# Attention block with resizing, one NeuronCore: the values of three batches in half-precision parts

## What is computed

```python
out = bilinear_resize(x, 64, 64)                       # 4096 positions, 256 channels
out = relu(bn(conv1x1(out, conv1_w), bn1_s, bn1_b))    # called a in the kernel
q, k = conv1x1(out, q_w, q_b), conv1x1(out, k_w, k_b)  # 32 channels each
v = conv1x1(out, v_w, v_b)                             # 256 channels
attn = softmax(einsum('bdi,bdj->bij', q, k), axis=-1)  # 4096 x 4096
out = gamma * einsum('bcj,bij->bci', v, attn) + out
out = bn(conv1x1(relu(bn(out, bn2_s, bn2_b)), conv2_w), bn3_s, bn3_b)
return relu(bilinear_resize(out, 128, 128) + x)
```

## Time and profile before

| | |
|---|---|
| median of 3 executions | 2367.78 us |
| the profiled execution | 2371.97 us |
| its span in the profile | 2370.2 us |
| granted TensorE clock, mean | 0.994 of full speed |
| PE busy | 2298.5 us (97%) |
| DVE busy | 1783.7 us (75%) |
| ACT busy | 1706.3 us (72%) |
| POOL busy | 1671.0 us (70%) |

### The profile page before, as it was taken

How to read it: one execution, slowest core, us unless ns; L and a number is a source line. 1 busy time by engine, 2 the same in 40 slices (tenths; PEclk the granted TensorE clock), 3 DMA queues, 4 the chain that set the end, 5 groups by cost and what they waited for, 6 DMA issues and landing times.

```text
span 2370.2 us, 48197 instructions
## 1 busy us (share of the span) xinstructions
PE 2298.5 (97%) x15970; PEld 1650.3 (70%) x15970; DVE 1783.7 (75%) x3294; ACT 1706.3 (72%) x3305; POOL 1671.0 (70%) x1610
## 2 busy tenths in 40 slices
PE   4799999999999999999999999999999999999998
PEld 2377777777667777777747777777775777777774
DVE  7666578887568888888657888888756777777778
ACT  5567777777657777777755777777765777777773
POOL 7992468888369988888728988889845454444464
PEclk8899999999999999999999999999999999999999
DMA  6321112322102332222301322233310112222322
GB/s 212 107 72 46 36 54 107 106 92 104 54 23 103 108 107 103 93 105 98 107 10 54 109 106 102 102 107 106 106 55 1 63 63 71 71 71 71 142 96 100
DMA packets 59273, 204.11 MB, mean 86 GB/s; under 512 B 8752, under 2 KB 9840, under 8 KB 59120
## 3 DMA queue, kind: packets, MB, share of 16 engines
q1 hardware_dynamic: 41696, 138.93, 18.2%
q10 hardware_dynamic: 17424, 63.45, 6.5%
HBM read 135.24 MB, written 67.11 MB: 85 GB/s over the span
## 4 chain that ended last, share of the span: by engine, by line
PE 88%; DVE 4%; ACT 3%; POOL 3%; issue 1%; SPq 1%; DMA 0%; DVEq 0%; ACTq 0%; POOLq 0%
PE acc L1139 19%; PE acc L1141 18%; PE acc L1140 18%; PE et L1015 10%; PE emx L1003 6%; PE wrk L1037 4%; PE acc L1065 4%; PE wrk L1003 3%; PE acc L1057 2%; PE wrk L1028 1%; DVE qs L768 1%; DVE ks L768 1%; PE acc L1049 1%; ACT qs L535 1%; ACT qs L534 1%
## 5 line engine op out<-in xcount | busy, mean ns | idle before, releaser
L1139 PE MATMUL acc<-vh,ph 128*128 128x257 f16 x4096 | 1120.1, 273 | 1.7 <-DVE vl L778 1.4
L1141 PE MATMUL acc<-vh,pl 128*128 128x257 f16 x4096 | 1116.2, 273 | 0.0
L1140 PE MATMUL acc<-vl,ph 128*128 128x256 f16 x4096 | 1110.9, 271 | 0.0
L463 ACT ACTIVATE ph<-et 128x512 f16<-128x512 f32 x1024 | 610.5, 596 | 301.8 <-PE et L1015 293.0
L727 DVE TENSOR_TENSOR pl<-et,ph 128x512 f16<-128x512 f32 x1024 | 700.6, 686 | 139.4 <-ACT et L464 135.8
L464 ACT ACTIVATE et<-et 128x512 f32<-128x512 f32 x1024 | 607.0, 593 | 0.0
L1140 PEld LDWEIGHTS acc<-vl,ph 128*128 128x128 f16 x4096 | 400.9, 98 | 277.4 <-issue 20.5
L1139 PEld LDWEIGHTS acc<-vh,ph 128*128 128x128 f16 x4096 | 400.2, 98 | 70.6 <-issue 11.0
L1141 PEld LDWEIGHTS acc<-vh,pl 128*128 128x128 f16 x4096 | 395.4, 97 | 56.2
L377 POOL TENSOR_TENSOR ct<-cd,uw 128x512 f32<-128x512 f32 x246 | 325.0, 1343 | 134.7 <-DVE xres L758 130.3
L1015 PE MATMUL et<-qs,ks 98*128 (+1 forms) x1024 | 390.2, 381 | 2.7 <-DVE pl L727 0.9
(11 more groups left out here) (142 smaller groups left out, 2673.0 us busy)
## 6 DMA issues: line engine op xcount, KB each, us to landing
xres<-in_x SPq DMA_DIRECT2D x139, 512.0 KB, 4.5
out<-xres ACTq DMA_DIRECT2D x121, 512.0 KB, 2.6
xin<-in_x SPq DMA_DIRECT2D x110, 512.0 KB, 3.7
xr<-in_x SPq DMA_DIRECT2D x7, 512.0 KB, 7.4
out<-xr SPq DMA_DIRECT2D x6, 512.0 KB, 2.6
out<-xr SPq DMA_DIRECT2D x2, 256.0 KB, 2.1
osb<-in_L_conv_conv_w SPq DMA_DIRECT2D x1, 256.0 KB, 7.7
osb<-in_L_conv_v_w SPq DMA_DIRECT2D x1, 256.0 KB, 7.8
```

The costliest lines, as they stand in the source:

```text
L463: ops.activation(ph[:, t % 4, :], et[t % 2][:, :], ACT.Exp)
L1139: mm(acc[it][:, 0:C + 1], ph[:, tt % 4, pt], vh[:, tt, 0:C + 1], start=tt == 0, stop=False)
L1140: mm(acc[it][:, 0:C], ph[:, tt % 4, pt], vl[:, tt, :], start=False, stop=False)
L1141: last = mm(acc[it][:, 0:C + 1], pl[:, tt % 4, pt], vh[:, tt, 0:C + 1], start=False, stop=tt == JT - 1)
```

## The change

For batches 2 to 4 (b = 1 to 3) the values are no longer float32 products. ACT writes a half-precision high part of the scaled `a` (`a_high`, two instructions of 512 columns per chunk, behind the chunk's second `conv1_out`), DVE the low part (`a_low`, two instructions, behind the last `max` unit of the step; that of chunk 7 behind the last `max` unit of all). Both lie in `xr`, over the rows that `conv1` has used. `values` then makes three half-precision products where there was one of float32. The scale of `a` has to be known before `a` is: it is bounded from the largest input row value. DVE takes the maxima of `xr` in the last block of a batch (`largest_z`, 8 instructions of 1024 elements at the steps of `T_Z`), PE sums over partitions at step 29 (`T_SIZE`), DVE works out the scale (`size_of_a`). The parts of the weights (`wvh`, `wvl`) and constants are made once, in batch 0, block 1, step 2 (`fixed_sizes`). POOL and the loads of the last shortcut rows wait for `values` before they write into `xr`. Names that are new: `a_part(ck, low, half)` is the place in `xr`.

```diff
             def blk(b, n, c):
                 if is_last(b, c):
-                    sp.wait_ge(c1_rdy, 2 * NB * B)
+                    sp.wait_ge(v_rdy, VU * B)
...
             # POOL, blk
+                        if j == 0 and b > 0:
+                            pool.wait_ge(v_rdy, b * VU + 2 * (n + 1))
                         dst = xr[:, bass.ds(n, 1), j % 2, (j // 2) * (DR // 2):(j // 2 + 1) * (DR // 2), :]
...
             # ACT
+            def a_high(b, ck):
+                if ck == 0:
+                    act.wait_ge(a_rdy, b)
+                for half in range(CH):
+                    last = ops.activation(a_part(ck, 0, half), a[:, half, ck * IB:(ck + 1) * IB], ACT.Copy,
+                                          scale=a_scale[:, half:half + 1])
+                last.then_inc(a_hi, 1)
...
                         conv1_out(b, i // 2, i % 2)
+                        if i % 2 and not is_first(b):
+                            act.wait_ge(c1_done, b * (2 * NB) + (i + 1))
+                            a_high(b, i // 2)
                         if i == 1 and not is_first(b):
                             for half in range(2):
                                 relu_h(b * NB - 1, half)
...
             # DVE
+            def a_low(b, ck):
+                dve.wait_ge(a_hi, (b - 1) * NB + (ck + 1))
+                for half in range(CH):
+                    last = ops.scalar_tensor_tensor(a_part(ck, 1, half), a[:, half, ck * IB:(ck + 1) * IB],
+                                                    a_scale[:, half:half + 1], a_part(ck, 0, half), ALU.mult, ALU.subtract)
+                last.then_inc(a_lo, 1)
+            def fixed_sizes():
+                for m, w in ((wv_max, wvt), (w1_max, w1t)):
+                    ops.tensor_reduce(m, w[:], AX.X, ALU.max, apply_absolute_value=True).then_inc(a_fixed, 1)
+                for m, i in ((abs_s, S1), (abs_b, B1)):
+                    ops.scalar_tensor_tensor(m, par[:, i, :], -1.0, par[:, i, :], ALU.mult, ALU.max).then_inc(a_fixed, 1)
...
+                for h in range(CH):
+                    ops.tensor_scalar(wvh[:, h, :], wvt[:, h, :], wv_inv[:, h:h + 1], None, ALU.mult).then_inc(a_fixed, 1)
+                dve.wait_ge(a_fixed, 8)
+                for h in range(CH):
+                    last = ops.scalar_tensor_tensor(wvl[:, h, :], wvt[:, h, :], wv_inv[:, h:h + 1], wvh[:, h, :], ALU.mult,
+                                                    ALU.subtract)
+                last.then_inc(a_known, 1)
+            def largest_z(b, ck):
+                dve.wait_ge(down_p, down_count(b + 1, PIECES * (ck + 1)))
+                ops.tensor_reduce(z_max[:, ck, :], xr[:, ck].rearrange("p h r c -> p h (r c)"), AX.X, ALU.max,
+                                  apply_absolute_value=True).then_inc(z_seen, 1)
...
+                    if g == 1 and t == T_FIXED:
+                        fixed_sizes()
+                    if c == NB - 1 and b < B - 1:
+                        if t in T_Z:
+                            largest_z(b, T_Z.index(t))
+                        if t == T_Z[-1]:
+                            size_of_z(b)
+                        if t == T_SIZE + 1:
+                            size_of_a(b)
...
             # PE
             def values(b, v):
+                if not is_first(b):
+                    pe.wait_ge(a_lo, (b - 1) * NB + (v // 2 + 1))
+                    if v == 0:
+                        pe.wait_ge(a_known, 1)
                 for jj in range(VB):
...
                     for h in range(CH):
+                        if not is_first(b):
+                            high, low = (a_part(jt // IT, i, h)[:, keys] for i in range(2))
+                            mm(out, high, wvh[:, h, :], start=h == 0, stop=False)
+                            mm(out, high, wvl[:, h, :], start=False, stop=False)
+                            last = mm(out, low, wvh[:, h, :], start=False, stop=h == CH - 1)
+                            continue
...
+                    if c == NB - 1 and t == T_SIZE and not (isinstance(b, int) and b == B - 1):
+                        pe.wait_ge(y_rdy, g * 2)
+                        pe.wait_ge(z_rdy, b + 1)
+                        for h in range(CH):
+                            last = mm(wrk[:, C + 1:C + 2], ones_p[:, :], z_all[:, h:h + 1], start=h == 0, stop=h == CH - 1)
+                        last.then_inc(z_sum, 1)
...
             # _sequence
-        seq += first + second + m[:3] + middle + m[3:] if vector else first + m[:2] + middle + m[2:3] + second + m[3:]
+        low = [("a_low", ck - 1)] if ck else []
+        seq += first + second + m[:3] + middle + m[3:] + low if vector else first + m[:2] + middle + m[2:3] + second + m[3:]
...
-        seq += [row, m[0], m[1], one, scale, m[2], qk, v[0], m[3], m[4], m[5], v[1], m[6], v[2], m[7], *v[3:6]]
+        seq += [row, m[0], m[1], one, scale, m[2], qk, v[0], m[3], m[4], m[5], v[1], m[6], v[2], m[7], ("a_low", NB - 1), *v[3:6]]
...
+T_FIXED = 2
+T_Z = (1, 3, 7, 10, 12, 19, 20, 26)
+T_SIZE = 29
```

More of the change, by code:

```diff
@@ L80, in attention_block_kernel @@
         w2t = sb("w2t", [P, CH, C])
+        wvh = sb("wvh", [P, CH, C], F16)
+        wvl = sb("wvl", [P, CH, C], F16)
+        zs = sb("zs", [P, 18])
+        wv_max, w1_max, wv_inv, abs_s, abs_b, z_all, a_scale = (zs[:, 2 * i:2 * i + 2] for i in range(7))
+        a_gain, a_rest, a_top, v_scale = (zs[:, 14 + i:15 + i] for i in range(4))
+        a_parts = sb("a_parts", [P, CH, 2])
+        z_max = sb("z_max", [P, NB, CH])
+        a_inv = sb("a_inv", [P, 1])
         wva = sb("wva", [P, CH, C])
@@ L206, in late_bank, with a_part @@
             return acc[i % 2 * 2 + part]
+        def a_part(ck, low, half):
+            return xr[:, ck].rearrange("p h r c -> p (h r c)").bitcast(F16)[:, (low * CH + half) * IB:(low * CH + half + 1) * IB]
         def last_bank(half):
@@ new lines, in size_of_a @@
+            def size_of_a(b):
+                dve.wait_ge(z_sum, b + 1)
+                if b == 0:
+                    dve.wait_ge(a_sum, 1)
+                    ops.tensor_scalar(zs[:, 14:16], wrk[:, C + 2:C + 4], 1e-30, None, ALU.max).then_inc(a_known, 1)
+                    dve.wait_ge(a_known, 2)
+                ops.tensor_scalar(a_top, wrk[:, C + 1:C + 2], a_gain, a_rest, ALU.mult, ALU.add).then_inc(z_step, 1)
+                dve.wait_ge(z_step, b * 4 + 2)
+                ops.reciprocal(a_inv[:], a_top).then_inc(z_step, 1)
+                dve.wait_ge(z_step, b * 4 + 3)
+                ops.tensor_scalar(a_scale, wv_max, a_inv[:], A_TOP, ALU.mult, ALU.mult).then_inc(a_rdy, 1)
+                ops.tensor_scalar(a_top, a_top, 1.0 / A_TOP, None, ALU.mult).then_inc(z_step, 1)
@@ L787, in enter @@
                         qk_low(b, i)
+                    elif kind == "a_low" and not is_first(b):
+                        a_low(b, i)
                     elif kind == "max":
@@ L968, in _ @@
             pe.wait_ge(size_part, 1)
-            mm(acc[3][:, 4 * D:4 * D + 2], ones_d[:, :], ws[:, :], start=True, stop=True).then_inc(size_sum, 1)
+            mm(acc[3][:, 4 * D:4 * D + 2], ones_p[0:D, :], ws[:, :], start=True, stop=True).then_inc(size_sum, 1)
             pe.wait_ge(wt_ok, 3)
@@ L1061, in values @@
             def values(b, v):
+                if not is_first(b):
+                    pe.wait_ge(a_lo, (b - 1) * NB + (v // 2 + 1))
+                    if v == 0:
+                        pe.wait_ge(a_known, 1)
                 for jj in range(VB):
                     jt = v * VB + jj
+                    out = acc[bank_of("values", v)][:, jj * C:(jj + 1) * C]
+                    keys = slice(jt % IT * P, (jt % IT + 1) * P)
                     for h in range(CH):
+                        if not is_first(b):
+                            high, low = (a_part(jt // IT, i, h)[:, keys] for i in range(2))
[3 more added lines that the diff above has]
+                            continue
                         last = mm(acc[bank_of("values", v)][:, jj * C:(jj + 1) * C], a[:, h, jt * P:(jt + 1) * P], wvt[:, h, :],
@@ L1166, in blk @@
                         shift_transposes(g + 1)
+                    if c == NB - 1 and t == T_SIZE and not (isinstance(b, int) and b == B - 1):
[4 more added lines that the diff above has]
+                        last.then_inc(z_sum, 1)
+                        if is_first(b):
+                            pe.wait_ge(a_size, 1)
+                            for h in range(CH):
+                                last = mm(wrk[:, C + 2:C + 4], ones_p[:, :], a_parts[:, h, :], start=h == 0, stop=h == CH - 1)
+                            last.then_inc(a_sum, 1)
             def batch(b):
```

29 lines of the change are left out of this document (25 added, 4 removed).

## The result

The changed kernel takes 2382.68 us (median; 2379.75 to 2384.51) against 2368.63 (2367.7 to 2370.28) for the kernel before, run beside it on the same chip: ratio 1.0055, interval 1.0043 to 1.0067. It is slower, by 14 us in the medians. The profiled executions, on which all that follows is built, stand at 2382.68 and 2371.97 us, 10.7 apart; the forecast had 9.1 for this difference. The two figures differ because the profiled execution of the kernel before lies 3.3 us above the median of those timed beside the changed kernel. The traces explain the 10.7; where the other 3.3 us lie no trace shows.

The account below looks back on a forecast made before the run. PE was taken as the bound, except in the entry chunks, a latency loop through DVE and ACT. Terms of +2.1 us a batch, three times +6.3, plus 2.8 once gave +9.1: 2381.1 profiled, 2377 median; range 2362 to 2387.

Parts of the forecast that it names:

- A unit of twelve records every 0.11 us: Values on PE: a unit as twelve half-precision records takes 1.32 us instead of 1.73, 0.41 less.
- The pair: The two `a_low` instructions of a chunk on DVE: 1.35 us alone, 2.65 taking turns with a busy POOL.
- Rounds: Entry-phase chunk loop: `a_low` beside POOL's key differences (chunks 1, 3, 5) delays three rounds by 0.8 us, +2.4 a batch.
- The two rivals without turns: `a_low` on DVE is not slowed by POOL: 2365.2 us (chance 0.20), or 2361 with small parts cheap (0.17).
- `a_low(6)`: On DVE ahead of the reduction of `am`, for which PE waits: nothing covers it, 1.6 us later.
- Values: The values units after `a_low(6)` and `a_low(7)` on DVE: the last ends at 706.35 against 708.13, -1.8 us a batch.
- Start: Batch start: ACT does `a_high(0)` ahead of two `relu_h` and `qk_high(0)`, +0.6 us a batch (0.3 to 0.8).
- Block 7 with PE's sums: Size of the rows: PE's sums at step 29 +0.6 us, DVE's eight reductions in block 7 +0.2, per batch.
- Tail: End of values: ACT has two exponentials before the last high part, +0.1 us a batch.
- the once-only sums: Batch 0: two more sums on PE at step 29, +0.6 us once.
- the burst: `fixed_sizes` on DVE in batch 0: 3.6 us, of which 1.3 covered before energies need the low part; +2.2 (1 to 3.5).

Follow-up runs that it names:

- the three placements: Changed kernel with `fixed_sizes` spread over eight steps, `a_low(6)` behind the bound row's reduction, `a_low(7)` behind values 9: 2363.57 us, ratio 0.9963 against the kernel before.

## Why the prediction was right, and where it was not

The outcome, slower by 0.55%, is as forecast, and so is the deciding mechanism. The size is 10.7 us for 9.1 between the profiled executions, and 14 for 9.1 between the medians: 2377 was given, 2382.68 measured. Point by point:

- *A unit of twelve records every 0.11 us*: so it is.
- *The pair*: forecast 1.35 alone and 2.65 beside POOL; measured 1.41 and 2.58 to 2.65. The Trainium skill's rule (page "SBUF — State Buffer", section "SBUF: two separate sides"), that a VectorE operation with two SBUF inputs and a GpSimd operation that reads SBUF exclude each other for a whole instruction, is borne out by these two durations, and L799, with one SBUF input, kept 0.74 beside POOL's differences. One SBUF input does not always free an operation: the copy L797 has only one, and it went from 0.28 to 0.55.
- *Rounds*: forecast 3 x 0.8, measured 2.39, and with the low parts left out it all comes back. The two rivals without turns fall with this.
- *`a_low(6)`*: forecast 1.6, measured 1.32.
- *Values*: forecast -1.8 with `a_low(6)` in it, so -3.4 without; measured -3.7.
- *Start*: forecast +0.6, measured +0.45. *Block 7 with PE's sums*: forecast 0.8, measured 0.7, 0.5 and 0.3. *Tail*: forecast +0.1, but the first product of block 0 follows the last record of values by 0.11 us, so there is no wait. The stretch behind it, to the first `conv2`, is -0.4 in batches 1 and 2 and +0.05 in batch 3, where nothing was forecast.
- Together, with the once-only sums and without the clock, these came to 2.2 us in three batches where 6.3 + 0.6 was forecast: 4.7 us too many. All but the rounds are off to the same side by some tenths.

What failed is a premise of the whole sum: that a wait costs its length. **The step that failed first is `a_low(6)`**, costed at 1.6 and nothing behind it. Its own length was nearly right, but with the 1.51 us ahead of it the wait drew the clock down, and the products behind it were longer: +5.9 us over three batches. With +1.7 at the start of batch 2 and +1.7 in the burst that makes 9.3 us of which the prediction has nothing. The wait is neither the whole cause nor a certain one: without it the clock still fell in two bounds of six (`a_low(6)` moved, and the three placements), and with it the clock held in two of three when the burst stood at step 12. **The second is the burst**: +2.2 from the path through the low part of the exponentials. At step 2 a residual stands behind it and ACT's `relu_h` behind that. Without the clock it was 3.3 there, which the version with float32 values shows directly, since it kept the clock. My estimate was right for step 12, at 2.0.

Against this stand the 4.7 us of the terms that were too high, and 4.2 us in the blocks, for which the forecast had nothing either. So the closeness of the total owes much to luck: 9.1 - 4.7 - 4.2 + 7.6 (clock in the entry phases) + 2.8 (burst, 5.0 for 2.2) = 10.6.

The blocks: in a slow one of the kernel before, DVE's addition of an enlarged piece took 1.54 us beside an operation of POOL; at the same step of the changed one, the second row here, POOL was elsewhere in its cycle.

```profile
886.00 1.54 DVE L758 CUSTOM_DVE_ANT_0 xres<-xres,ct 128x512 f32<-128x512 f32 x1
...
892.54 0.91 DVE L789 CUSTOM_DVE_ANT_0 xres<-xres,ct 128x512 f32<-128x512 f32 x1
```

That the turns make the 0.25 us a block is argued from this pair of rows and not shown. What sets POOL's phase is open: the added wait was excluded. Nor is it clear that the 4.2 us belong to the change. In batch 0, from the first `conv2` to the last pair, the kernel before took 364.1 us and the changed one 363.2, but nine other versions, whose blocks of batch 0 are the changed ones, took 364.2, and the kernel before with POOL's wait, which acts only from batch 1 on, took 363.3. In batches 1 and 2 the versions with half-precision values and their low parts were all quicker than the kernel before, but the one with float32 values was not (370.6 us over six blocks of batch 1, where the kernel before took 370.4 and the changed one 369.2), which fits the rival that the start of a batch sets the phase. It was not tested.

## What to carry to other kernels

An operation that fits into an engine's idle time still costs what stands behind it in that engine's queue: the same instructions cost 0.55% where they were put first, and gained 0.37% once they were spread out or put behind the reduction and the evictions that others waited for. Price a wait of TensorE at its length, and then look whether the clock holds: add the products behind it at the lower level as a term of its own. Two operations with two SBUF inputs on VectorE beside a busy GpSimd should be priced at up to twice their time (2.65 for 1.41 us), and moving GpSimd out of the way moves the clash to the next pair unless the whole round is looked at.

## What the runs showed of the hardware that was not expected

- The granted clock fell to 0.50 in all three bounds of the changed kernel, after two idle times of 1.51 and 1.65 us with two short products between; the version with the burst at step 12 had the same idle times and lost it in one bound of three. After 1.51 and 0.32 it fell in two bounds of six. The kernel before, with 0.30 and 0.32 ahead of the bound, shows 1.00. So the same wait may be charged or not, and the price in the changed kernel was 1.6 or 1.7 us in most places and 2.6 once.
- Products that nobody reads, 2.2 us of them a batch, in those idle times kept it at 1.00 in all three batches and took 5.9 us off the bounds.
- DVE's pair beside POOL does not slow POOL's first operation (1.15), which was running already, but the second and the third (1.60 and 1.48 for 1.14 alone). Each engine's instruction ended before the other's went on: turns go by whole instructions on both sides.
- DVE's copy L797, 32x512 in half precision with one SBUF input, took 0.28 us alone and 0.55 beside POOL.
